# First feed-forward stage of a four-layer gated decoder: the recurrence's products, sums and ratio from VectorE to GpSimd, norms scaled by a broadcast operand, and results turned at another place in TensorE's queue

## The chip, the core and the metric

The kernel runs on one core of a Trainium2 chip. The metric is device time in microseconds (us) of one execution. The core has five instruction queues that run side by side and meet at semaphores: PE (TensorE, matmuls and transposes), DVE (VectorE), ACT (ScalarE), POOL (GpSimd) and SP (which only issues DMAs here). Each queue is in order: an instruction that waits holds up everything behind it on its own engine.

## The reference

Eight sequences (B = 8) of 256 tokens with 512 features pass four layers; each layer adds a gated attention-like part and a gated feed-forward part to `x`. The stage in question computes two additions at once:

```python
x = x + tanh(g_ffn[0])   * L0_ffn(layernorm(x), W_up, W_gate, W_down)      # 512 -> 2048 -> 512, ternary weights, silu gate
x = x + tanh(g_xattn[1]) * wkv(w, u, k=layernorm(x), v=ctx)                # after the line above
# wkv, per channel, over the 256 time steps:
no = max(o, u + k);   A = exp(o - no);      E = exp(u + k - no)
y  = (A*p + E*v) / (A*q + E)
no2 = max(w + o, k);  A2 = exp(w + o - no2); E2 = exp(k - no2)
p, q, o = A2*p + E2*v, A2*q + E2, no2
```

## The kernel before

The stage is written as one function per engine (`pool_stage12`, `pe_stage12`, `act_stage12`, `dve_stage12`, from line 793), and each engine's order is written out by hand. An outer loop runs over the 8 sequences `b`; an inner one over `j` = 0 to 7, eight slices of 256 of the 2048 hidden features. For one slice:

- PE, `up_gate(b, j)` (L829): 32 matmuls of 128x256 for the up and the gate product, into one of two pairs of PSUM banks. It waits until `hid` of slice j-2 is computed, since that frees the banks.
- ACT takes tanh of the first half (L931); DVE makes `hid` in two operations (L1066, L1068; the text calls the pair "hid j"); ACT rounds it to fp16 (L934, "high j"); DVE makes the fp16 rest (L1088, "low j"), which waits for high j.
- PE, `down(b, j)` (L816): 8 matmuls of 128x512. Down j is issued behind up_gate j+2 and waits for low j.

Between these, each slice carries pieces of three other jobs. In the pass over sequence b they are, by their place before the change:

1. Norm and keys of sequence b-1 (its feed-forward result has just been added): sums at DVE j = 0 (`norm_sums`, L749, L753), the power -1/2 on POOL (L169, L170), scaling at DVE j = 0 behind low 0 (`norm_apply`, L758, two operations for two tiles of 128 tokens), turning on PE at j = 1 and 2 (`keys`, L744), copying on ACT at j = 1 and 2 (`key_copy`, L890), then the running maximum (DVE j = 4, L1028), the differences (j = 5, L1039), ReLU and exp on ACT (j = 6, 7 and 0; L899 to L921), and the scans for q and p (L1047, L1049 at j = 7, L1058 behind the loop over j).
2. The quotient of sequence b-2: three products (`products`, L989 to L991, DVE j = 1), two sums (`totals`, L997, L999, j = 2), reciprocal in halves (`invert`, L1006, j = 3 and 6), and the ratio (L1012, j = 7).
3. The result of sequence b-3 is turned back on PE (`y_back`, L839, at j = 0 and 2) and added to x (`add_y`, L1019, DVE j = 1 and 3).

The norm of sequence b+1 for its own feed-forward pass runs beside them: sums at DVE j = 2, scaling at j = 3, the two tiles are turned on PE at j = 4 and 6 through PSUM bank 0, copied by ACT in the same j (`ffn_high`, L763) and by DVE at j = 5 and 7 (`ffn_low`, L768). All turns through bank 0 form one chain: each waits on `front_bank_free`, the count of tiles already taken out of the bank. Behind the loop over j, DVE adds the feed-forward result to x (L1108) once `down(b, 7)` is done.

After the pass over b = 7 the same jobs are finished for sequences 5 to 7 in a tail that DVE leads, up to the norm for the next stage (`NEXT`).

A few helpers: `dc.step` counts an instruction on a semaphore, `settle` waits until all counted ones are complete, `link` is both. `front_rstd` (L167) is the pair L169, L170.

Of the kernel before, what the change touches and what calls it, by code (L numbers as in the profile page):

```python
# [13 lines left out]
ALU = mybir.AluOpType  # L14
# [51 lines left out]
def build(nc, t):  # L66
# [3 lines left out]
    with ctx:  # L70
# [684 lines left out]
        def norm_apply(dve, f, xi):  # L755
            dve.wait_ge(sig("front_rstd"), f + 1)
            for t_ in range(TT):
                nc.vector.tensor_scalar(xn[:, f % 2, t_, :], X[:, xi * TT + t_, :], mv[:, t_, 0:1], rstd[:, t_:t_ + 1],  # L758
                                        ALU.subtract, ALU.mult).then_inc(sig("xn_ready"), 1)

# [32 lines left out]
        def pool_stage12(pool, pc):  # L793
            def rstd_of(f):
                front_rstd(pool, pc, None, f % 8, f // 8)

            rstd_of(front_of_ffn(0))
            for b in range(B + 2):
                if 1 <= b <= B:
                    rstd_of(front_of_wkv(b - 1))  # L800
                if b + 1 < B:
                    rstd_of(front_of_ffn(b + 1))
                if b == B:
                    rstd_of(NEXT)
                    rstd_of(NEXT + 1)

        def pe_stage12(pe):
# [41 lines left out]
            for b in range(B):  # L849
                f = front_of_ffn(b)  # L850
                pe.wait_ge(sig("front_bank_free"), tile_no(f, TT))
                for j in range(NJ):
                    if b == 0 and j < 2:
                        pe.wait_ge(sig("conv_added"), B + 3 + 2 * j)
                    if b == 0 and j == 2:
                        pe.wait_ge(sig("conv_added"), NTILES)
                    up_gate(b, j)
                    if j == 0:
                        y_back(b - 3, 0)
                    if j == 1:  # L860
                        keys(b - 1, 0)
                    if j == 2:
                        y_back(b - 3, 1)
                        keys(b - 1, 1)
                    if j in (4, 6) and b + 1 < B:
                        transpose_front(pe, front_of_ffn(b + 1), j // 2 - 2)
                    if j >= 2:
                        down(b, j - 2)
                down(b, NJ - 2)
                down(b, NJ - 1)  # L870
            y_back(B - 3, 0)
            keys(B - 1, 0)
# [10 lines left out]
        def act_stage12(act):  # L883
# [43 lines left out]
            for b in range(B):  # L927
                for j in range(NJ):
# [7 lines left out]
                    if j == 0:  # L936
                        present_exp(b - 2)
                    if j in (1, 2):
                        key_copy(b - 1, j - 1)
                    if j in (1, 2, 3, 5, 6):  # L940
                        sum_later(act, 5 * b + (1, 2, 3, 5, 6).index(j))
                    if j in (4, 6) and b + 1 < B:
                        ffn_high(act, front_of_ffn(b + 1), (b + 1) % 2, j // 2 - 2)
                    if j == 6:
# [22 lines left out]
        def dve_stage12(dve, dc, conv_add):  # L967
# [14 lines left out]

            def products(c):
                if c < 0:
                    return
                dve.wait_ge(sig("wkv_exp_ready"), 2 * c + 2)
                dve.wait_ge(sig("wkv_pq_ready"), KD * (c + 1))
                dc.settle()
                dc.step(nc.vector.tensor_tensor(wk_den, wk_d[:, 0], wk_q[:, :, 0:S], ALU.mult))  # L989
                dc.step(nc.vector.tensor_tensor(wk_num, wk_d[:, 0], wk_p[:, :, 0:S], ALU.mult))  # L990
                nc.vector.tensor_tensor(wk_ev, wk_d[:, 1], wk_v, ALU.mult).then_inc(sig("wkv_ev_ready"), 1)  # L991

            def totals(c):
                if c < 0:
                    return
                dc.settle()
                nc.vector.tensor_tensor(wk_den, wk_den, wk_d[:, 1], ALU.add).then_inc(sig("wkv_den_ready"), 1)  # L997
                dve.wait_ge(sig("wkv_ev_ready"), 2 * c + 2)
                nc.vector.tensor_tensor(wk_num, wk_num, wk_ev, ALU.add).then_inc(sig("wkv_den_ready"), 1)  # L999

            def invert(c, half):
                if c < 0:
                    return
                dve.wait_ge(sig("wkv_den_ready"), 2 * c + 2)
                part_ = wk_den[:, 2 * half:2 * half + 2, :]
                dc.step(nc.vector.reciprocal(part_, part_))  # L1006

            def ratio(c):
                if c < 0:
                    return  # L1010
                dc.settle()
                nc.vector.tensor_tensor(wk_y, wk_num, wk_den, ALU.mult).then_inc(sig("wkv_y_ready"), 1)  # L1012
# [29 lines left out]
            def weights_scan(c):  # L1042
                if c < 0:
                    return
                dve.wait_ge(sig("wkv_exp_ready"), 2 * c + 1)
                dve.wait_ge(sig("wkv_v_loaded"), 16 * (c + 1))
                nc.vector.tensor_tensor(wk_ev, wk_d[:, 3], wk_v, ALU.mult).then_inc(sig("wkv_ev_ready"), 1)  # L1047
                for k in range(KD):
# [12 lines left out]
            for b in range(B):  # L1061
                for j in range(NJ):
# [7 lines left out]
                    if j == 0 and b:  # L1070
                        dve.wait_ge(sig("ffn0_added"), TT * b + TT)
                        norm_sums(dve, dc, front_of_wkv(b - 1), b - 1)
                    if j == 1:
                        products(b - 2)
                    if j == 2:
                        totals(b - 2)
                    if j == 3:
                        invert(b - 2, 0)
                    if j == 4:
                        running_max(b - 1)  # L1080
                    if j in (5, 7) and b + 1 < B:
# [31 lines left out]
            norm_apply(dve, front_of_wkv(c), c)  # L1113
            products(c - 1)
            add_y(c - 2, 0)
            totals(c - 1)
            add_y(c - 2, 1)
# [4 lines left out]
            invert(c - 1, 1)  # L1122
            ratio(c - 1)
            dve.wait_ge(sig("wkv_added"), TT + TT * (c - 1))
# [2296 lines left out]
```

## Time and profile before

| | us |
|---|---|
| median of three runs | 3336.74 (3334.93 to 3345.0) |
| the profiled execution's own time | 3338.15 |
| its span, first to last instruction | 3336.4 |
| the stage's loop, first to last up_gate matmul | 334.0 to 735.5 |
| the stage's tail, to about | 812 |

Busy shares of the whole span are PE 87%, DVE 75%, ACT 52%, POOL 28%. They average over seven stages with different limits. The pass over one sequence takes about 50 us, and the eight passes together 12% of the span. In the timeline views a row's first number is the start in us from the span's start and the second the duration; the number in brackets is how long the engine stood idle before it, and behind the arrow whose work it waited for. Instructions on one engine overlap slightly at their ends, so that a row of 0.69 us costs its queue about 0.6.

### The profile page before, as it was taken

Reading aid. Unit: us, or ns where it says so; the run is one execution under the profiler, and the core shown is the slowest. Engines: PE = TensorE matmul, PEld = TensorE weight load, DVE = VectorE, ACT = ScalarE, POOL = GpSimd, SP = SyncE. Lnnn points to the kernel's source line nnn. Section 1 sums busy time; section 2 is a strip of 40 time slices with the busy share of each in tenths; the row PEclk is TensorE's granted clock in tenths of the full one; section 3 lists DMA queues with packets and bytes.
Section 4 is the critical chain, followed back from the end, with each engine's and each line's share of the span. In section 5 each row is a group of like instructions: output and inputs, shape, how many; then the busy total and the mean of one; then the engine's idle time right before and its main releaser. Section 6 shows DMA issues by size and latency. Waiting matters only on the chain.

```text
span 3336.4 us, 48456 instructions
## 1 busy us (share of the span) xinstructions
PE 2912.3 (87%) x18346; PEld 1702.2 (51%) x18346; DVE 2497.5 (75%) x4554; ACT 1724.1 (52%) x2659; POOL 923.7 (28%) x1359
## 2 busy tenths in 40 slices
PE   8999988883789898668888667999999999998999
PEld 4444766652444444456666433555455445444666
DVE  7887589988766666788888768777777777766433
ACT  3331344444265554079998864454444544445444
POOL 5543000002200000046776774222222222211000
PEclk9999999996899999889999878999999999999999
DMA  7422221212110102100000021000000000011000
GB/s 250 142 98 74 65 63 58 64 49 85 31 27 24 27 17 73 48 26 1 1 1 1 24 80 57 1 7 7 1 7 7 1 7 7 1 47 59 13 14 26
DMA packets 60421, 132.78 MB, mean 40 GB/s; under 512 B 6496, under 2 KB 27808, under 8 KB 59424
## 3 DMA queue, kind: packets, MB, share of 16 engines
q1 hardware_dynamic: 50976, 96.11, 9.3%
q10 hardware_dynamic: 9216, 33.56, 3.3%
q8 instruction: 150, 2.46, 0.3%
q14 instruction: 79, 0.65, 0.1%
HBM read 119.03 MB, written 4.19 MB: 37 GB/s over the span
## 4 chain that ended last, share of the span: by engine, by line
PE 60%; DVE 23%; ACT 9%; issue 4%; POOL 3%; DMA 0%; DVEq 0%; ACTq 0%; SPq 0%; POOLq 0%
PE psum L1269 10%; PE psum L660 8%; PE psum L2237 5%; PE psum L2767 4%; PE psum L3238 3%; PE psum L3216 3%; PE psum L2726 3%; ACT area_g L2312 3%; PE psum L829 3%; PE psum L2751 3%; PE psum L2118 2%; PE psum L2736 2%; PE psum L2258 2%; DVE area_a L1876 2%; PE psum L1524 2%
## 5 line engine op out<-in xcount | busy, mean ns | idle before, releaser
L2312 ACT ACTIVATE area_g<-area_a 128x2048 bf16<-128x2048 f32 x168 | 334.7, 1996 | 32.1 <-POOL area_a L2181 22.9
L2237 PE MATMUL psum<-area_c,ident_bf 128*128 128x128 bf16 x3328 | 234.2, 236 | 93.7 <-DVE area_c L2346 93.7
L660 PE MATMUL psum<-area_b,area_g 128*128 128x512 f32 x640 | 280.9, 595 | 2.1 <-issue 2.1
L2237 PEld LDWEIGHTS psum<-area_c,ident_bf 128*128 128x128 bf16 x3328 | 218.9, 107 | 119.6 <-DVE area_c L2346 112.4
L169 POOL TENSOR_TENSOR rstd<-mean_var,eps_col 128x2 f32<-128x2 f32 x56 | 19.0, 339 | 938.0 <-DVE mean_var L753 498.1
L829 PE MATMUL psum<-xT_high,area_a 128*128 128x256 f16 x1024 | 236.9, 280 | 1.4 <-DVE xT_low L768 1.4
L2726 PE MATMUL psum<-area_b,stage 128*128 128x512 f32 (+1 forms) x512 | 237.5, 546 | 0.0
L829 PE MATMUL psum<-xT_low,area_a 128*128 128x256 f16 x1024 | 236.5, 280 | 0.0
L2878 ACT ACTIVATE xn<-psum,small 128x384 f32<-128x384 f32 (+1 forms) x256 | 163.8, 640 | 96.1 <-DVE small L3017 95.9
L3017 DVE TENSOR_REDUCE small<-psum 128x1 f32<-128x384 f32 (+1 forms) x256 | 158.3, 618 | 71.6 <-PE psum L2727 69.2
L2643 POOL TENSOR_TENSOR small<-small,half_pow 128x4 f32<-128x4 f32 x96 | 131.7, 1372 | 273.9 <-DVE small L2964 273.9
L660 PEld LDWEIGHTS psum<-area_b,area_g 128*128 128x128 f32 x640 | 120.7, 191 | 148.1 <-issue 144.1
L2751 PE MATMUL psum<-area_g,area_a 128*128 128x512 f16 x672 | 166.2, 381 | 29.5 <-DVE area_g L3030 24.3
L2887 ACT ACTIVATE area_g<-psum 128x384 f16<-128x384 f32 (+1 forms) x256 | 139.3, 544 | 93.0 <-PE psum L2736 91.4
L2177 POOL TENSOR_SCALAR area_a<-area_a 128x1 f32<-128x1 f32 x224 | 130.9, 584 | 184.5 <-ACT area_g L2312 175.9
L2635 POOL TENSOR_TENSOR stage<-area_g 128x256 f32<-128x256 f32 x79 | 58.7, 742 | 441.0 <-ACT area_g L2860 311.8
L1269 PE MATMUL psum<-area_c,xT_high 128*128 128x512 f16 x512 | 178.7, 391 | 0.0
L1876 DVE TENSOR_REDUCE area_a<-psum 128x2 bf16<-128x512 f32 x256 | 163.4, 682 | 15.7 <-PE psum L1483 15.4
L479 POOL TENSOR_TENSOR area_b<-area_b,area_c 128x512 f32<-128x512 f32 x128 | 139.6, 1122 | 118.5 <-PE psum L660 112.5
L3023 DVE RECIPROCAL small<-small 128x1 f32<-128x1 f32 x256 | 41.6, 163 | 168.3 <-ACT xn L2878 165.4
L2736 PE MATMUL psum<-ident,xn 128*128 128x128 f32 x896 | 145.7, 280 | 19.8 <-DVE xn L3024 19.0
L3030 DVE SCALAR_TENSOR_TENSOR area_g<-psum,area_g 128x384 f16<-128x384 f32 (+1 forms) x256 | 157.9, 617 | 0.8 <-ACT area_g L2887 0.8
(423 smaller groups left out, 7490.7 us busy)
## 6 DMA issues: line engine op xcount, KB each, us to landing
stage<-in_w ACTq DMA_DIRECT2D x24, 512.0 KB, 4.4
stage<-in_w SPq DMA_DIRECT2D x24, 512.0 KB, 3.6
area_g<-in_toeplitz SPq DMA_DIRECT2D x32, 256.0 KB, 2.7
area_b<-in_ctxT SPq DMA_DIRECT2D x15, 512.0 KB, 3.9
area_b<-area_b SPq DMA_DIRECT2D x24, 256.0 KB, 3.7
stage<-in_ctxT SPq DMA_DIRECT2D x9, 512.0 KB, 4.0
x_stream<-in_x SPq DMA_DIRECT2D x4, 1024.0 KB, 8.1
area_c<-in_ctxT SPq DMA_DIRECT2D x8, 512.0 KB, 7.5
```

The costliest lines, as they stand in the source:

```text
L660: last = nc.tensor.matmul(psum[:, bank + m, :], toep[:, h % 2, (m - k) * P:(m - k + 1) * P], kv[:, h % 2, k, :], start=(k == 0), stop=(k = ...
L829: last = nc.tensor.matmul(out, w[:, k, m * P:(m + 1) * P], xt[:, b % 2, k, :], start=(k == 0 and n == 0), stop=(k == KD - 1 and n == 1))
L1269: r = nc.tensor.matmul(out, u, v, start=(first and n == 0), stop=(last_ and n == 2))
L1876: nc.vector.tensor_reduce(max4[:, st % 2, 4 * u + 2 * n:4 * u + 2 * n + 2], src, AX.X, ALU.max, negate=True).then_inc(sig("max4_ready"), 1)
L2237: last = nc.tensor.matmul(psum[:, 1, t_ * P:(t_ + 1) * P], identb[:, :], above5[:, t_, c * P:(c + 1) * P], start=(c == 0), stop=(c == KE - 1))
L2312: nc.scalar.activation(junk5[t_], z5[b % 3][:, t_, :], ACT.Sign, bias=fine5[:, par, t_:t_ + 1], scale=-1.0, accum_out=signs5[:, t_:t_ + 1] ...
L2726: nc.tensor.matmul(psum[:, 2 + n % 2, 0:nk], qT6[:, u % 2, h, :], kT6[:, b % 2, 0:nk // P, g, :], start=True, stop=False)
L2736: last = nc.tensor.transpose(psum[:, 4 + n % 2, k * P:(k + 1) * P], p6[:, n % 2, k * P:(k + 1) * P], ident[:, :])
L2751: last = nc.tensor.matmul(psum[:, 6, :], v6[:, b % 2, k, vp, g * P:(g + 1) * P], pT6[:, pp, k, :], start=(vp + pp + k == 0), stop=(pp == 1 ...
L2878: nc.scalar.activation(p6[:, n % 2, 0:nk], psum[:, 2 + n % 2, 0:nk], ACT.Exp, bias=nmax6[:, n % 2:n % 2 + 1], scale=-1.0, accum_out=sum6[: ...
L3017: nc.vector.tensor_reduce(nmax6[:, n % 2:n % 2 + 1], psum[:, 2 + n % 2, 0:nk], AX.X, ALU.min).then_inc(sig("nmax6_ready"), 1)
L3030: nc.vector.scalar_tensor_tensor(out=pT6[:, 1, 0:nb, h * P:(h + 1) * P], in0=psum[:, 4 + n % 2, 0:nb * P].rearrange("p (n q) -> p n q", q= ...
```

## The change

POOL receives `denominator`, `numerator` and `ratio` for sequences 0 to 6 (six operations of 128x1024), placed between the two norms' powers of a pass; DVE keeps only the reciprocals, now at j = 1 and 2. For the last sequence DVE keeps the denominator and the ratio, and POOL makes the numerator. The norm's scaling is a `scalar_tensor_tensor` whose second tensor operand is `rstd` broadcast along 512 elements, where it was a `tensor_scalar`. On PE, keys move from j = 1, 2 to j = 2, 3; the turns for the next feed-forward pass from j = 4, 6 to j = 5, 6; the turn-back of tile 0 from j = 0 of the pass b+3 to the place before the last down product of the pass b+2. ACT's and DVE's partner operations move with them: `ffn_low` from j = 5, 7 to j = 6, 7, the second norm's sums and scaling from j = 2, 3 to j = 3, 4, `add_y` of tile 0 from j = 1 to j = 0.

```diff
@@ norm_apply
-                nc.vector.tensor_scalar(xn[:, f % 2, t_, :], X[:, xi * TT + t_, :], mv[:, t_, 0:1], rstd[:, t_:t_ + 1],
-                                        ALU.subtract, ALU.mult).then_inc(sig("xn_ready"), 1)
+                nc.vector.scalar_tensor_tensor(out=xn[:, f % 2, t_, :], in0=X[:, xi * TT + t_, :], scalar=mv[:, t_, 0:1],
+                                               in1=rstd[:, t_:t_ + 1].broadcast_to([P, D]), op0=ALU.subtract,
+                                               op1=ALU.mult).then_inc(sig("xn_ready"), 1)
@@ pool_stage12
+            def denominator(c):
...
+                pool.wait_ge(sig("wkv_exp_ready"), 2 * c + 2)
+                pool.wait_ge(sig("wkv_pq_ready"), KD * (c + 1))
...
+                pc.link(nc.gpsimd.tensor_tensor(wk_den, wk_d[:, 0], wk_q[:, :, 0:S], ALU.mult))
+                nc.gpsimd.tensor_tensor(wk_den, wk_den, wk_d[:, 1], ALU.add).then_inc(sig("wkv_den_ready"), 1)
+            def numerator(c):
...
+                pc.step(nc.gpsimd.tensor_tensor(wk_num, wk_d[:, 0], wk_p[:, :, 0:S], ALU.mult))
+                nc.gpsimd.tensor_tensor(wk_ev, wk_d[:, 1], wk_v, ALU.mult).then_inc(sig("wkv_ev_ready"), 1)
+                pc.settle()
+                pool.wait_ge(sig("wkv_ev_ready"), 2 * c + 2)
+                nc.gpsimd.tensor_tensor(wk_num, wk_num, wk_ev, ALU.add).then_inc(sig("wkv_den_ready"), 1)
+            def ratio(c):
...
+                pool.wait_ge(*after("wkv_inverted", 2 * c + 2))
+                pool.wait_ge(sig("wkv_den_ready"), 2 * c + 2)
...
+                nc.gpsimd.tensor_tensor(wk_y, wk_num, wk_den, ALU.mult).then_inc(sig("wkv_y_ready"), 1)
...
                 if 1 <= b <= B:
                     rstd_of(front_of_wkv(b - 1))
+                    denominator(b - 2)
+                    numerator(b - 2)
+                    ratio(b - 2)
@@ pe_stage12, behind up_gate(b, j)
-                    if j == 0:
-                        y_back(b - 3, 0)
-                    if j == 1:
-                        keys(b - 1, 0)
                     if j == 2:
                         y_back(b - 3, 1)
-                        keys(b - 1, 1)
-                    if j in (4, 6) and b + 1 < B:
-                        transpose_front(pe, front_of_ffn(b + 1), j // 2 - 2)
+                    if j in (2, 3):
+                        keys(b - 1, j - 2)
+                    if j in (5, 6) and b + 1 < B:
+                        transpose_front(pe, front_of_ffn(b + 1), j - 5)
                     if j >= 2:
                         down(b, j - 2)
                 down(b, NJ - 2)
+                y_back(b - 2, 0)
                 down(b, NJ - 1)
@@ act_stage12
-                    if j in (1, 2):
-                        key_copy(b - 1, j - 1)
+                    if j in (2, 3):
+                        key_copy(b - 1, j - 2)
...
-                    if j in (4, 6) and b + 1 < B:
-                        ffn_high(act, front_of_ffn(b + 1), (b + 1) % 2, j // 2 - 2)
+                    if j in (5, 6) and b + 1 < B:
+                        ffn_high(act, front_of_ffn(b + 1), (b + 1) % 2, j - 5)
@@ dve_stage12, between hid j and low j
-                    if j == 1:
-                        products(b - 2)
-                    if j == 2:
-                        totals(b - 2)
-                    if j == 3:
-                        invert(b - 2, 0)
...
-                    if j in (5, 7) and b + 1 < B:
-                        ffn_low(dve, (b + 1) * TT + (j - 5) // 2 + 1, (b + 1) % 2, (j - 5) // 2)
-                    if j == 6:
-                        invert(b - 2, 1)
-                    if j == 7:
-                        ratio(b - 2)
+                    if j in (6, 7) and b + 1 < B:
+                        ffn_low(dve, (b + 1) * TT + j - 5, (b + 1) % 2, j - 6)
@@ dve_stage12, behind low j
-                    if j in (1, 3):
-                        add_y(b - 3, j // 2)
-                    if j == 2 and b + 1 < B:
+                    if j in (0, 3):
+                        add_y(b - 3, j // 3)
+                    if j in (1, 2):
+                        invert(b - 2, j - 1)
+                    if j == 3 and b + 1 < B:
                         norm_sums(dve, dc, front_of_ffn(b + 1), b + 1)
-                    if j == 3 and b + 1 < B:
+                    if j == 4 and b + 1 < B:
                         norm_apply(dve, front_of_ffn(b + 1), b + 1)
```

In the tail the same functions leave DVE's queue; `last_denominator(7)` and `last_ratio(7)` stay on it, and `numerator(7)` is POOL's last piece of the stage.

## Rows read from the trace of the kernel before

**Rows 1.** The page, busy time, share and instructions of each engine over the span.

```profile
PE 2912.3 (87%) x18346; PEld 1702.2 (51%) x18346; DVE 2497.5 (75%) x4554; ACT 1724.1 (52%) x2659; POOL 923.7 (28%) x1359
```

**Rows 2.** Windows: length, busy us (instructions) of PE, PEld, DVE, ACT, POOL, clock, DMA.

```profile
334.00:384.00 50.00, 50.00 (x379) 38.07 (x380) 24.59 (x42) 17.32 (x30) 0.89 (x2) 0.96 0.20 63
484.00:534.00 50.00, 43.39 (x314) 31.40 (x313) 45.34 (x67) 24.83 (x36) 2.14 (x4) 0.97 0.20 64
```

**Rows 3.** Timeline of DVE, pass b = 3: start, us, instruction, idle before, releaser.

```profile
482.79 0.68 DVE L1066 SCALAR_TENSOR_TENSOR area_b<-area_b,psum 128x512 f32<-128x512 f32 x1
...
487.22 1.00 DVE L758 TENSOR_SCALAR xn<-x_stream,mean_var,rstd 128x512 f32<-128x512 f32 x2 [0.86 <-POOL rstd L170]
488.13 0.68 DVE L1066 SCALAR_TENSOR_TENSOR area_b<-area_b,psum 128x512 f32<-128x512 f32 x1
489.45 1.22 DVE L989 TENSOR_TENSOR area_c<-area_c,area_b 128x1024 f32<-128x1024 f32 x1
...
502.08 3.35 DVE L1006 RECIPROCAL area_c<-area_c 128x512 f32<-128x512 f32 x1
...
508.77 2.43 DVE L1028 TENSOR_TENSOR_SCAN area_b<-scalars,area_b 128x256 f32<-128x256 f32 x4
...
513.11 0.69 DVE L1066 SCALAR_TENSOR_TENSOR area_b<-area_b,psum 128x512 f32<-128x512 f32 x1 [1.33 <-PE psum L829]
...
515.22 0.69 DVE L1088 SCALAR_TENSOR_TENSOR area_b<-area_b 128x512 f16<-128x512 f32 x1
515.83 3.25 DVE L1039 SCALAR_TENSOR_TENSOR area_c<-area_b,scalars 128x256 f32<-128x256 f32 x8
...
525.08 0.69 DVE L1066 SCALAR_TENSOR_TENSOR area_b<-area_b,psum 128x512 f32<-128x512 f32 x1 [0.88 <-ACT area_b L931]
...
528.99 1.23 DVE L1047 TENSOR_TENSOR stage<-area_c,stage 128x1024 f32<-128x1024 f32 x1 [0.16 <-ACT area_c L906]
...
536.25 0.68 DVE L1066 SCALAR_TENSOR_TENSOR area_b<-area_b,psum 128x512 f32<-128x512 f32 x1
```

**Rows 4.** Timeline of PE, pass b = 3, columns as in rows 3.

```profile
487.82 0.89 PE L744 MATMUL psum<-ident,xn 128*128 128x128 f32 x4 [3.08 <-DVE xn L758]
491.72 0.27 PE L829 MATMUL psum<-xT_high,area_a 128*128 128x256 f16 x1
496.99 0.27 PE L829 MATMUL psum<-xT_high,area_a 128*128 128x256 f16 x1
500.48 1.89 PE L816 MATMUL psum<-area_a,area_b 128*128 128x512 f16 x8
507.13 0.66 PE L744 MATMUL psum<-ident,xn 128*128 128x128 f32 x4 [1.27 <-DVE xn L758]
```

**Rows 5.** Timeline of ACT, pass b = 3, columns as in rows 3.

```profile
484.76 1.89 ACT L921 ACTIVATE area_c<-area_c 128x2048 f32<-128x2048 f32 x1
514.56 0.63 ACT L934 ACTIVATE area_b<-area_b 128x512 f16<-128x512 f32 x1 [2.57 <-DVE area_b L1068]
527.07 1.89 ACT L906 ACTIVATE area_c<-area_c 128x2048 f32<-128x2048 f32 x1
```

**Rows 6.** By source line: durations ns min/median/max, first and last start.

```profile
L491 POOL TENSOR_TENSOR area_g<-area_a,area_g x16: 1259/1268/1272, 28.8 to 175.5; 128x512 f32<-128x512 f32 x16
L2635 POOL TENSOR_TENSOR stage<-area_g x79: 722/725/1701, 2005.2 to 3068.3; 128x256 f32<-128x256 f32 x79
```

**Rows 7.** Timeline of DVE and POOL where both read SBUF, three places elsewhere.

```profile
154.04 1.66 DVE L556 SCALAR_TENSOR_TENSOR x_stream<-area_g,gates,x_stream 128x512 f32<-128x512 f32 x1
154.09 1.06 POOL L479 TENSOR_TENSOR area_b<-area_b,area_c 128x512 f32<-128x512 f32 x1
155.11 1.51 POOL L479 TENSOR_TENSOR area_b<-area_b,area_c 128x512 f32<-128x512 f32 x1
...
777.80 0.96 POOL L170 TENSOR_TENSOR rstd<-rstd,half_pow 128x2 f32<-128x2 f32 x1
...
795.70 2.49 POOL L1177 TENSOR_TENSOR x_stream<-x_stream,area_g 128x512 f32<-128x512 f32 x2
```

More of the change, by code:

```diff
@@ L127, in sig, with reused, after @@
             return sems[name]
+        REUSED = {"wkv_inverted": ("kv_ready", KD * HC)}
+        def reused(name):
+            return sig(REUSED[name][0])
+        def after(name, n):
+            return sig(REUSED[name][0]), REUSED[name][1] + n
         def at(i, par, per, k):
@@ L795, in rstd_of @@
                 front_rstd(pool, pc, None, f % 8, f // 8)
+            def denominator(c):
+                if c < 0:
+                    return
+                pool.wait_ge(sig("wkv_exp_ready"), 2 * c + 2)
+                pool.wait_ge(sig("wkv_pq_ready"), KD * (c + 1))
+                if c:
+                    pool.wait_ge(sig("wkv_y_ready"), c)
+                pc.link(nc.gpsimd.tensor_tensor(wk_den, wk_d[:, 0], wk_q[:, :, 0:S], ALU.mult))
+                nc.gpsimd.tensor_tensor(wk_den, wk_den, wk_d[:, 1], ALU.add).then_inc(sig("wkv_den_ready"), 1)
+            def numerator(c):
+                if c < 0:
+                    return
+                pool.wait_ge(sig("wkv_exp_ready"), 2 * c + 2)
+                pool.wait_ge(sig("wkv_pq_ready"), KD * (c + 1))
+                if c:
+                    pool.wait_ge(sig("wkv_y_ready"), c)
+                pc.step(nc.gpsimd.tensor_tensor(wk_num, wk_d[:, 0], wk_p[:, :, 0:S], ALU.mult))
[4 more added lines that the diff above has]
+            def ratio(c):
+                if c < 0:
+                    return
+                pool.wait_ge(*after("wkv_inverted", 2 * c + 2))
+                pool.wait_ge(sig("wkv_den_ready"), 2 * c + 2)
+                if c:
+                    pool.wait_ge(sig("wkv_yT_ready"), TT * c)
+                nc.gpsimd.tensor_tensor(wk_y, wk_num, wk_den, ALU.mult).then_inc(sig("wkv_y_ready"), 1)
             rstd_of(front_of_ffn(0))
@@ L805, in pool_stage12 @@
                     rstd_of(NEXT + 1)
+            numerator(B - 1)
         def pe_stage12(pe):
@@ L869, in pe_stage12 @@
                 down(b, NJ - 2)
+                y_back(b - 2, 0)
                 down(b, NJ - 1)
-            y_back(B - 3, 0)
             keys(B - 1, 0)
@@ L981, in dve_stage12, with last_denominator @@
                 dc.step(nc.vector.memset(z[:, :, 0:1], v))
-            def products(c):
-                if c < 0:
-                    return
+            def last_denominator(c):
                 dve.wait_ge(sig("wkv_exp_ready"), 2 * c + 2)
                 dve.wait_ge(sig("wkv_pq_ready"), KD * (c + 1))
[L988 to L999, printed above, removed]
+                dve.wait_ge(sig("wkv_y_ready"), c)
+                dc.link(nc.vector.tensor_tensor(wk_den, wk_d[:, 0], wk_q[:, :, 0:S], ALU.mult))
+                dc.link(nc.vector.tensor_tensor(wk_den, wk_den, wk_d[:, 1], ALU.add))
+                dve.sem_inc(sig("wkv_den_ready"), 1)
             def invert(c, half):
@@ L1003, in invert, with last_ratio @@
                     return
-                dve.wait_ge(sig("wkv_den_ready"), 2 * c + 2)
[L1005 to L1011, printed above, removed]
+                if c < B - 1:
+                    dve.wait_ge(sig("wkv_den_ready"), 2 * c + 1)
+                part_ = wk_den[:, 2 * half:2 * half + 2, :]
+                nc.vector.reciprocal(part_, part_).then_inc(reused("wkv_inverted"), 1)
+            def last_ratio(c):
+                dve.wait_ge(*after("wkv_inverted", 2 * c + 2))
+                dve.wait_ge(sig("wkv_den_ready"), 2 * c + 2)
                 nc.vector.tensor_tensor(wk_y, wk_num, wk_den, ALU.mult).then_inc(sig("wkv_y_ready"), 1)
@@ L1046, in weights_scan @@
                 dve.wait_ge(sig("wkv_v_loaded"), 16 * (c + 1))
+                if c:
+                    dve.wait_ge(sig("wkv_den_ready"), 2 * c)
                 nc.vector.tensor_tensor(wk_ev, wk_d[:, 3], wk_v, ALU.mult).then_inc(sig("wkv_ev_ready"), 1)
@@ L1113, in dve_stage12 @@
             norm_apply(dve, front_of_wkv(c), c)
-            products(c - 1)
             add_y(c - 2, 0)
-            totals(c - 1)
             add_y(c - 2, 1)
@@ L1122, in dve_stage12 @@
             invert(c - 1, 1)
-            ratio(c - 1)
             dve.wait_ge(sig("wkv_added"), TT + TT * (c - 1))
@@ L1133, in dve_stage12 @@
             sums34(dve, dc)
-            products(c)
-            totals(c)
+            last_denominator(c)
             squares_to_pool(dve, dc)
@@ L1139, in dve_stage12 @@
             invert(c, 1)
-            ratio(c)
+            last_ratio(c)
             for t_ in range(TT):
```

## The prediction

> **What bounds the kernel now.** The page's busy shares [rows 1] average seven stages and say nothing of this one, so I went to the windows. In the pass over b = 0 PE is busy all the time, 50.0 of 50 us; in the pass b = 3 no engine is, PE 43.4 and DVE 45.3, and POOL works 2.1 us [rows 2]. A stage in which nobody is full is bound by a chain that changes engines, and that is read from the timelines, engine by engine. I take the pass b = 3 and count from its hid 0 at 482.79; the next pass's hid 0 starts at 536.25, so a pass lasts 53.46 us [rows 3]. What ends last in it:
>
> - DVE, from 0 to about 24.3: the norm, hid, products, sums and reciprocal, up to the scaling that PE waits for at 507.13 (1.27 us) [rows 4].
> - PE from 24.3 to hid 7 at 42.29: DVE waits for it twice, 1.33 us at 513.11 and 0.88 us at 525.08, there with ACT's tanh in between [rows 3].
> - From hid 7 to the next hid 0, 11.17 us: hid and low 7, then the history product L1047, the scans and the sum onto x. L1047 waits for an exp of ACT [rows 3, 5].
> - PE also loses time early on: it waits 3.08 us for the scaled norm at 487.82, and restarts at the slow one of its two levels (four turns in 0.89 us against 0.66 at 507.13), back at full speed by 491.7 [rows 4]. That is some 3.9 us at half speed, 1.9 us lost, so 5.0 in all. It is not on the chain of this pass: DVE's hid 3 comes later anyway.
>
> **Prices.** hid costs DVE 1.32 (487.22 + 1.00 to 489.45, less overlap), low 0.60 (515.22 to 515.83), a product or sum of 1024 elements 1.14 (1.22 less the overlap of 0.08), a reciprocal half 3.26, running maximum 2.35, differences 3.17 [rows 3]. up_gate costs PE 3.49 (496.99 to 500.48), a down 1.73 (1.89 less overlap), four turns 0.47 (0.66 less overlap) [rows 4].
>
> **What DVE loses and gains per pass.** Off its queue: 3 products, 2 sums, 1 ratio, 6 x 1.14 = 6.8 us. But the ratio stood where DVE would wait otherwise: with hid 7 at 525.08, high 7 and the exp at 527.07 to 528.96 [rows 5], L1047 can't start before 528.99 in either version. So the stretch from hid 7 to the next hid 0 stays 11.17, and 5.7 us remain. Against it:
>
> 1. low j waits for ACT's high j. From the start of hid to that of low are 2.11 us (513.11 to 515.22), although only 1.32 + 0.6 of work lay between [rows 3]. Before, every slice had a filler there. After, j = 1, 2, 3 and 5 have none (the reciprocals now stand behind low), and each costs 2.11 - 1.32 = 0.79 idle, 3.2 us in all.
> 2. The scaling with two tensor operands: no such row exists. The old pair cost 1.00 less overlap, 0.91 [rows 3], which is the lower end; the upper is 2 x 0.69, the row of low, which is the nearest: the same instruction, two SBUF tensors, 512 elements. It costs its queue 0.60, so I take 1.2 a pair: +0.3, twice a pass.
> 3. The scaling for the next feed-forward pass moves behind hid 4, running maximum and low 4, and behind both reciprocals instead of one.
>
> **POOL's six operations.** None of 128x1024 is in the trace. Two inputs of 512 elements take 1.268 us, of 256 elements 0.725 [rows 6]: 0.543 per 256 more, so 1.268 + 2 x 0.543 = 2.35 us. Bounds: 2.1 (twice the 1.06 of L479 in rows 7) and 2.6. Six are 14.1 us on an engine that has 2.1 us of work, and the quotient isn't needed before the next pass. By load this is free; the price is what they do to DVE. The Trainium skill (GPSIMD Engine Reference, Instruction dispatch) gives some 2.5 cycles an element at 1.2 GHz for two inputs; my estimate from it is 2.13 us, and the sum would shrink by a tenth.
>
> **DVE and POOL exclude each other.** At 154.04 DVE's L556, which reads two SBUF tensors, takes 1.66 us; it ends with 0.6 us of work behind POOL's L479, which ran from 154.09 to 155.15, and POOL's next one, started at 155.11, takes 1.51 instead of 1.06 [rows 7]. Each was held for the other's whole instruction, then they alternate: L170 at 777.80, among four scans of DVE, takes 0.96, one scan's rest and not four. L1177 meanwhile runs twice in 2.49, full speed, beside a reciprocal of DVE [rows 7]: one with a single input doesn't count. The Trainium skill (SBUF — State Buffer, Who interferes with whom) has this as a rule: a DVE instruction with two SBUF inputs contends with a GpSimd one that reads SBUF, and the first holds the pair of ports for the whole instruction. It speaks against this change, as the new scaling falls under it just as the old did; the trace agrees, with the 1.66 us.
>
> Which DVE work meets POOL's? Scaling (two SBUF tensors), low (two), not hid or add_y (PSUM and SBUF), not the reciprocal. POOL is free at 4.4, when its power is done (that releases the scaling, at 487.22, rows 3), and the exp it needs ended before that, 484.76 + 1.89 = 486.65 [rows 5]. The walk, with POOL's work P1 to P6:
>
> - If DVE's scaling takes the pair first: scaling 0 4.43-5.05, P1 5.05-7.4, scaling 1 7.4-8.0, P2 8.0-10.35, add_y and hid 1 from 8.0 to 10.0, low 1 wanted at 10.8, held by P3 until 12.7, ends 13.3, reciprocal to 16.6, hid 2 and low 2 to 19.3, reciprocal to 22.5, hid 3, low 3 wanted at 24.6, held by P6 until 24.95, ends 25.55.
> - If P1 is first: scaling 0 held until 6.75, scaling 1 until 9.75 (P2 gets in between), low 1 until 15.1, low 3 ends at 27.95.
> - Without exclusion low 3 ends at 21.24 by the same walk.
>
> So exclusion costs 4.3 or 6.7 us a pass. P1 and the scaling are released by the same instruction, so I can't say which wins.
>
> **What PE does.** It no longer waits for the keys at j = 1. But a turn through bank 0 waits for the tile before it to leave the bank. Turn 1 of the next pass stands behind up_gate 6; tile 0 leaves with `ffn_low` at DVE's j = 6, behind hid 6, and hid 6 waits for up_gate 6. Before, `ffn_low` was at j = 5, a slice ahead. PE now stands still from the end of up_gate 6 until hid 6 and ffn_low are done: 0.3 + 1.32 + 0.68 = 2.3 us, in every pass with a next one, and up_gate 7 and hid 7 with it.
>
> From low 3 on: add_y 0.66, sums 1.58, hid 4, maximum, low 4, 6.5 to the scaling, at 27.75 without exclusion, PE's turn at 28.5, its queue has waited 2.4 us. hid 5, low 5, differences: DVE reaches hid 6 at 34.83; PE has finished up_gate 6 at 34.2. ffn_low ends 36.8, turn 1, down 4, up_gate 7: 36.9 + 0.47 + 1.73 + 3.49 = 42.6, hid 7 at 42.84. Before it was 42.29. So without exclusion a pass lasts 54.0, +0.5: what DVE saves it spends waiting, 5.3 us of it before hid 7. With exclusion it is 58.3 or 60.7, +4.8 or +7.2.
>
> **The sum.** b = 0, PE-bound: +2.3 (turn 1). b = 1, no quotient yet: the 3.08 + 1.9 before the keys go, turn 1 costs 2.3, other waits 0.7: -2. b = 2 to 6: 5 x 4.8 = 24 or 5 x 7.2 = 36. b = 7 has no next pass, so neither turn 1 nor the second scaling to wait for: the 4.3 or 6.7 of exclusion less some 3.5 that DVE sheds there, +1 or +3. Tail: DVE sheds 6 x 1.14 for sequence 6 and 3 x 1.14 for sequence 7, 10.3 us, but its scans and differences, all with two SBUF inputs, alternate with P1 to P5 of 2.35 each from 751 on, and the product L1047 with the ratio: I take 0, between -6 and +6. Sum: 2.3 - 2 + 24 + 1 = +25 or 2.3 - 2 + 36 + 3 = +39, middle +32. On the profiled execution's 3338.15 that is 3370; its time is 1.4 above the runs' median, so against them **3369**, with 3354 to 3382 as this case's own range.
>
> **The rivals.**
>
> - *Exclusion is short* (POOL lets DVE in between its reads, or the long tiles fall into gaps): the walk with 54.0 a pass, b = 2 to 6 5 x 0.5, b = 7 -3.5, b = 0 and 1 nothing together: -1, about 3336. For it: a held DVE was only seen with 512-element tiles. Against: 1.66 for 0.6.
> - *PE was the bound, faster*: PE gets back the 5.0 us before the keys in each pass from 1 to 7 and DVE's 5.7 us let it. It holds if DVE reaches hid 6 and ffn_low early enough that the chain is DVE's alone: 53.46 - 5.7 + 0.6 + 3.2 less its waits for PE and tanh of 1.33 and 0.88 is 49.4 a pass, -4.1 in six: -25, 3312. It decides from where turn 1's wait is shorter than 2.3 minus what PE is ahead. Against: that wait is set by hid 6 of the same slice, whatever DVE's load.
> - *The clock falls as well*: PE waits 2.7 us or more before turn 0 and 3.5 before turn-back 1; at 3.08 it came back slow [rows 4]. 1.75 us more in each of five passes on top of P1 first: 39 + 9 = +48, 3385.
>
> **Chances.** Forecast 0.52, short exclusion 0.2, PE the bound 0.17, clock 0.11. The runs tell no change within 0.3%, 10 us. Slower by more: 0.51 of the first, all of the last, little of the second: 0.64. Within: 0.18. Faster: 0.18. Range 3322 to 3387; what it leaves out is most of the faster rival.
>
> **What would show it.** Rows on POOL of about 2.35 us; DVE's scaling and low 1 with durations of 1.5 to 3 us instead of 0.6 (if they stay 0.7, exclusion is refuted); PE idle 2.3 us at the second turn, released by ffn_low L768; no 3.08 us wait at keys; 5 us of DVE idle before hid 7; spacing of hid 0 near 58 to 61 us. A spacing under 53 refutes the forecast.

## The result, and the profile after

The changed kernel takes 3396.63 us (median of 4 runs, 3394.83 to 3398.03) against 3338.22 us for the kernel before, measured beside it. The ratio is 1.0172 with a 95% interval of 1.0160 to 1.0184: slower by 58 us, where I had forecast slower by 32 (3369, range 3322 to 3387). The direction was right, the size was not, and the time lies outside the range.

The spans differ by 59.8 us (3396.2 against 3336.4). The page after, busy us and shares as in [rows 1]:

```profile
PE 2933.0 (86%) x18346; PEld 1710.0 (50%) x18346; DVE 2507.1 (74%) x4509; ACT 1723.3 (51%) x2659; POOL 1037.2 (31%) x1404
```

POOL has 113 us more. DVE lost 45 instructions and is busy *longer*, 2507.1 against 2497.5 us: time in which it is held counts as busy. That is the first thing to see; the busy share of a held engine hides the wait.

DVE's timeline, one pass (b = 3) from hid 0 at 498.62 (start, us, instruction, idle before); it answers to [rows 3]:

```profile
498.62 0.68 DVE L1102 SCALAR_TENSOR_TENSOR area_b<-area_b,psum 128x512 f32<-128x512 f32 x1
...
503.06 5.39 DVE L768 SCALAR_TENSOR_TENSOR xn<-x_stream,mean_var,rstd 128x512 f32<-128x512 f32 x2 [0.87 <-POOL rstd L180]
508.37 0.74 DVE L1053 SCALAR_TENSOR_TENSOR x_stream<-psum,gates,x_stream 128x512 f32<-128x512 f32 x1
...
511.12 2.23 DVE L1114 SCALAR_TENSOR_TENSOR area_b<-area_b 128x512 f16<-128x512 f32 x1 [0.70 <-ACT area_b L978]
513.28 3.34 DVE L1041 RECIPROCAL area_c<-area_c 128x512 f32<-128x512 f32 x1
...
524.50 1.02 DVE L1114 SCALAR_TENSOR_TENSOR area_b<-area_b 128x512 f16<-128x512 f32 x1 [0.70 <-ACT area_b L978]
...
531.91 1.41 DVE L768 SCALAR_TENSOR_TENSOR xn<-x_stream,mean_var,rstd 128x512 f32<-128x512 f32 x2
...
548.88 0.69 DVE L1102 SCALAR_TENSOR_TENSOR area_b<-area_b,psum 128x512 f32<-128x512 f32 x1 [6.99 <-PE psum L876]
```

The same scaling pair L768 takes 5.39 us at 503.06, beside POOL's work, and 1.41 at 531.91, without it. Low 1 (511.12) takes 2.23 and low 3 1.02, where a free one takes 0.69. The reciprocal is 3.34 as before. Then DVE stands idle 6.99 us before hid 7.

POOL in that pass; of these rows only the power L180 has a counterpart before. The products, sums and the ratio are the prediction's P1 to P6:

```profile
502.32 0.70 POOL L180 TENSOR_TENSOR rstd<-rstd,half_pow 128x2 f32<-128x2 f32 x1
502.99 2.17 POOL L815 TENSOR_TENSOR area_c<-area_c,area_b 128x1024 f32<-128x1024 f32 x1
505.24 2.67 POOL L816 TENSOR_TENSOR area_c<-area_c 128x1024 f32<-128x1024 f32 x1
507.86 2.62 POOL L825 TENSOR_TENSOR area_c<-area_c,area_b 128x1024 f32<-128x1024 f32 x1
510.46 2.35 POOL L826 TENSOR_TENSOR stage<-area_c,stage 128x1024 f32<-128x1024 f32 x1
512.95 2.62 POOL L829 TENSOR_TENSOR area_c<-area_c,stage 128x1024 f32<-128x1024 f32 x1
522.61 2.36 POOL L838 TENSOR_TENSOR area_g<-area_c 128x1024 f32<-128x1024 f32 x1 [7.05 <-DVE area_c L1041]
```

POOL's first product starts at 502.99, before the scaling that the same power released (503.06): P1 went first. The 5.39 us are P1 to 505.16, scaling 0, P2 to 507.91, scaling 1. Undisturbed P2, P4, P5 and P6 take 2.35 to 2.36 and P3 takes 2.17 (as in number 7), so that P2 and P5 carry 0.3 and P3 0.45 us of waiting for DVE.

PE, same pass, to [rows 4] (turn 0 and turn 1 are the transposes of the two tiles of the next feed-forward norm):

```profile
509.26 1.09 PE L886 MATMUL psum<-ident,area_g 128*128 128x128 f32 x4 [5.51 <-DVE x_stream L1053]
...
532.71 0.66 PE L754 MATMUL psum<-ident,xn 128*128 128x128 f32 x4 [2.46 <-DVE xn L768]
533.20 1.89 PE L863 MATMUL psum<-area_a,area_b 128*128 128x512 f16 x8
...
541.25 1.08 PE L754 MATMUL psum<-ident,xn 128*128 128x128 f32 x4 [2.67 <-DVE xT_low L779]
542.13 3.15 PE L863 MATMUL psum<-area_a,area_b 128*128 128x512 f16 x8
```

PE waits 5.51 us for add_y (before: 3.08 for the keys), 2.46 at turn 0 and 2.67 at turn 1, released by ffn_low L779. Behind the last of these the eight down matmuls take 3.15 us instead of 1.89. The windows behind turn 1 and behind turn 0 (columns as in [rows 2]) show why: granted clock 0.51, the slower of the two levels, against 1.00.

```profile
541.25:544.70 3.45, 3.45 (x11) 1.72 (x12) 0.64 (x1) 3.28 (x5) 0.00 (x0) 0.51 0.50 152
532.71:536.00 3.29, 3.29 (x22) 2.24 (x23) 2.56 (x5) 1.33 (x2) 0.00 (x0) 1.00 0.06 17
```

The slow stretch behind turn 1 is on the chain, since DVE has nothing left to do before hid 7. The one behind the 5.51 us is not: DVE starts hid 3 at 522.45 without a wait for PE.

The profile's view of the chain that ended last passes the sums of the keys' norm in every pass, so their starts in that view give the pass lengths. Before and after, for b = 2 and b = 3:

```profile
432.64 1.21 DVE stats L749 x2
484.19 1.21 DVE stats L749 x2
...
537.65 1.21 DVE stats L749 x2
```

```profile
438.78 1.21 DVE stats L759 x2
...
500.02 1.21 DVE stats L759 x2
...
561.44 1.21 DVE stats L759 x2
```

51.55 and 53.46 us before, 61.24 and 61.42 after. All of it in one table, read from the same chain:

| stretch | before | after | more | forecast, P1 first |
|---|---|---|---|---|
| start of the loop | 334.0 | 336.3 | +2.4 | 0 |
| b = 0 up to the sums | 49.7 | 52.0 | +2.3 | +2.3 |
| b = 1 | 48.95 | 50.46 | +1.5 | -2 |
| b = 2 | 51.55 | 61.24 | +9.7 | +7.2 |
| b = 3 to 6, each | 53.5 | 61.4 | +7.9 | +7.2 |
| b = 7 | 49.8 | 53.9 | +4.1 | +3 |
| tail, to the sums at 814.05 and 870.61 | 65.9 | 71.0 | +5.1 | 0 |
| the rest of the kernel | | | +3.2 | 0 |

The tail's rows show the holds once more. On the chain stand two scaling pairs of 5.41 and 5.31 us (1.41 without POOL's work, as number 1 below shows), the running maximum with 5.31 (2.44) and the history product with 2.07 (1.22), 11.6 us in all:

```profile
802.40 5.41 DVE L768 SCALAR_TENSOR_TENSOR xn<-x_stream,mean_var,rstd 128x512 f32<-128x512 f32 x2 [1.09 <-POOL rstd L180]
811.22 5.31 DVE L1062 TENSOR_TENSOR_SCAN area_b<-scalars,area_b 128x256 f32<-128x256 f32 x4 [0.73 <-ACT area_b L934]
```

### The profile page after: what moved, and what is told of

Same layout as the page of the kernel before. It is cut to its first block, busy times and chain, and to the rows that moved or that the text cites. A ratio compares the mean times of both kernels' runs of the same rounds, so it can differ in the third digit from the quotient of the medians.

```text
span 3396.2 us, 48481 instructions
## 1 busy us (share of the span) xinstructions
PE 2933.0 (86%) x18346; PEld 1710.0 (50%) x18346; DVE 2507.1 (74%) x4509; ACT 1723.3 (51%) x2659; POOL 1037.2 (31%) x1404
## 3 DMA queue, kind: packets, MB, share of 16 engines
q8 instruction: 150, 2.46, 0.3%
## 4 chain that ended last, share of the span: by engine, by line
PE 57%; DVE 25%; ACT 9%; issue 5%; POOL 2%; DMA 0%; DVEq 0%; ACTq 0%; SPq 0%; POOLq 0%
PE psum L1293 10%; PE psum L670 8%; PE psum L2261 5%; PE psum L2791 4%; PE psum L3262 3%; PE psum L3240 3%; ACT area_g L2336 3%; PE psum L2750 3%; PE psum L2775 3%; PE psum L2142 3%; PE psum L2760 2%; PE psum L2282 2%; DVE area_a L1900 2%; PE psum L876 2%; PE psum L1548 2%
## 5 line engine op out<-in xcount | busy, mean ns | idle before, releaser
L876 PE MATMUL psum<-xT_high,area_a 128*128 128x256 f16 x1024 | 228.7, 274 | 3.2 <-DVE xT_low L779 1.4
L876 PE MATMUL psum<-xT_low,area_a 128*128 128x256 f16 x1024 | 228.4, 274 | 0.0
L978 ACT ACTIVATE area_b<-area_b 128x512 f16<-128x512 f32 x64 | 40.3, 630 | 233.2 <-DVE area_b L1104 233.2
```

The lines of the kernel that those rows point to most:

```text
L876: last = nc.tensor.matmul(out, w[:, k, m * P:(m + 1) * P], xt[:, b % 2, k, :], start=(k == 0 and n == 0), stop=(k == KD - 1 and n == 1))
```

## The experiments

Times are medians; ratios are against the kernel before measured alongside, with 95% intervals. "Pass" is the length of a pass from b = 3 on. Each edit is on the changed kernel unless it says otherwise.

**1. POOL's operations made tiny** (same instructions, waits and places).

```diff
-pc.link(nc.gpsimd.tensor_tensor(wk_den, wk_d[:, 0], wk_q[:, :, 0:S], ALU.mult))
+pc.link(nc.gpsimd.tensor_tensor(wk_den[:, :, 0:1], wk_d[:, 0, :, 0:1], wk_q[:, :, 0:1], ALU.mult))
...
```

> The changed kernel, with POOL's six operations of a pass cut to one column of each 256 (128x4 elements instead of 128x1024); all waits and places stay. The rest of each tile of numerator, denominator and y is left out, so y is not the recurrence's. Theory (POOL's long operations hold DVE, 6 to 7 us a pass, and PE's turn waits are the rest): the scaling pair falls from 5.4 to 1.3 us, low 1 from 2.2 to 0.7, low 3 from 1.0 to 0.7, a pass from 61.4 to about 54 to 55.5, the time from 3397 to about 3350 (6 passes x 6.5, and some 5 of the tail). Rival (the moved turns on PE are the cause, POOL's work hides beside them): a pass stays near 60, the time above 3385.

3346.08 us, ratio 1.0014 (1.0004 to 1.0023), passes of 53.9 and 55.5. So the length of POOL's operations makes about 50 of the 58 us. DVE's scaling in it:

```profile
496.01 1.41 DVE L768 SCALAR_TENSOR_TENSOR xn<-x_stream,mean_var,rstd 128x512 f32<-128x512 f32 x2 [0.86 <-POOL rstd L180]
...
500.10 0.69 DVE L1114 SCALAR_TENSOR_TENSOR area_b<-area_b 128x512 f16<-128x512 f32 x1 [0.70 <-ACT area_b L978]
```

1.41 instead of 5.39 and low 1 0.69 instead of 2.23, with the same instructions queued. The passes are near the walk without exclusion, 54.0; the granted clock is 0.97 in the passes of 53.9 and 0.94 in those of 55.5. With DVE relieved of the whole quotient and POOL costing next to nothing, a pass is no shorter than before, nor than with the moved places alone (54.9, number 5). The same with the places left as before was not run. The tail is 59.3 us here, 6.6 less than before and 11.7 less than after.

**2. POOL waits for the scaling.**

```diff
                     rstd_of(front_of_wkv(b - 1))
+                    pool.wait_ge(sig("xn_ready"), tile_no(front_of_wkv(b - 1), TT - 1))
                     denominator(b - 2)
```

> The changed kernel, where POOL's first product of a pass waits until DVE has scaled both tiles of the keys' norm (one wait more on POOL, before denominator). Theory (who takes the ports first decides): the scaling pair takes 1.3 instead of 5.4 us, keys and hid 1 come 4 us earlier, but low 1 and low 2 now meet P2 and P5, so a pass gains about 2 of them: 59.5 us, time about 3385. Rival (each held instruction simply moves to the next one, the sum of held time is constant): no gain, 3397. Rival 2 (all 4 us stay gained): 3373.

3379.67 us, ratio 1.0119 (1.0102 to 1.0136): 17 us gained, passes of 57.6 and 59.0. Between the theory's 12 and rival 2's 24. DVE:

```profile
496.51 1.41 DVE L768 SCALAR_TENSOR_TENSOR xn<-x_stream,mean_var,rstd 128x512 f32<-128x512 f32 x2 [0.87 <-POOL rstd L180]
...
500.60 2.57 DVE L1115 SCALAR_TENSOR_TENSOR area_b<-area_b 128x512 f16<-128x512 f32 x1 [0.70 <-ACT area_b L979]
...
508.40 2.17 DVE L1115 SCALAR_TENSOR_TENSOR area_b<-area_b 128x512 f16<-128x512 f32 x1 [0.70 <-ACT area_b L979]
```

The scaling is free, low 1 is held 0.3 longer than in the changed kernel and low 2, free there (0.69), now meets P5: 4.0 gained, 1.8 handed back.

**3. Turn 1 a slice later**, which leaves its PSUM bank time to be emptied.

```diff
-                    if j in (5, 6) and b + 1 < B:
-                        transpose_front(pe, front_of_ffn(b + 1), j - 5)
+                    if j in (5, 7) and b + 1 < B:
+                        transpose_front(pe, front_of_ffn(b + 1), (j - 5) // 2)
... (ACT the same; ffn_low of tile 1 behind low 7)
```

> The changed kernel with the turn of tile 1 of the next feed-forward norm behind up_gate 7 instead of up_gate 6 (PE and ACT at j = 7), its ffn_low behind low 7. Tile 0's ffn_low at j = 6 is then done before PE reaches the turn. Theory: PE's 2.67 us wait before the second turn and the slow clock behind it (down 4 in 3.15 instead of 1.89) go, 3.5 to 4 us in each of seven passes with a next one, less 0.6 for the copy now ahead of the exp: 3.2 x 7 = 22, time about 3375, DVE's idle before hid 7 falls from 7.0 to about 3. Rival (the stretch from hid 7 to the next hid 0, with scans on DVE, sets the period): under 5 us gained.

3374.68 us, ratio 1.0098 (1.0081 to 1.0115): 22 us, as expected, with passes of 57.8 to 59.0. DVE's idle time before hid 7 falls from 6.99 to 2.82 us. The pass b = 1, which has no quotient, falls from 50.5 to 47.0: 3.5 us for this one wait and the slow clock behind it.

**4. The old form of the scaling.**

```diff
-nc.vector.scalar_tensor_tensor(out=xn[...], in0=X[...], scalar=mv[...], in1=rstd[...].broadcast_to([P, D]), ...)
+nc.vector.tensor_scalar(xn[...], X[...], mv[...], rstd[...], ALU.subtract, ALU.mult)
```

> The changed kernel with the norm's scaling as tensor_scalar again. Theory (both forms are held by POOL alike; the form costs 0.2 to 0.4 us a pair more): scaling pair beside POOL still about 5 us, other pairs 1.0 instead of 1.4, time 0.4 x 8 + 0.4 x 8 + some 3 in the next stage less, if on the chain: 3390. Rival (the new form is what is held, the old one passes): the pair takes 1.0 beside POOL, a pass gains 4, time about 3370.

3387.90 us, ratio 1.0140 (1.0124 to 1.0157), 9 us less than the changed kernel. Free pairs are 1.00, the held one is still long:

```profile
497.65 4.86 DVE L768 TENSOR_SCALAR xn<-x_stream,mean_var,rstd 128x512 f32<-128x512 f32 x2 [0.87 <-POOL rstd L180]
```

The new form bought nothing beside POOL and costs 0.4 a pair everywhere else, also in the next stage. The row also corrects a reading of the prediction, that an instruction "with a single input doesn't count": this form reads one tensor beside its two columns of scalars, and it is held all the same. What the reciprocals show holds for the reciprocals.

**5. The moved places alone** (on the kernel before: keys at j = 2, 3, turns at 5, 6, turn-back 0 before the last down product, partners with them).

> The kernel before with only the places moved (keys to j = 2, 3, the next norm's turns to j = 5, 6, turn-back 0 before the last down product, the DVE and ACT partners with them); products, sums, reciprocals and ratio stay on DVE at their old places, scaling as before. Theory (the turns' waits are a cost of their own): PE waits for ffn_low before its second turn, 2.3 to 2.7 us with a slow clock behind it, and the second scaling stands a slice later; a pass lasts 55.5 to 57 instead of 53.5, time about 3352. Rival (the moved places cost only together with POOL's work): 3340. Rival 2 (PE's 3.08 us wait at the keys was on the chain): below 3330.

3348.81 us, ratio 1.0027 (1.0016 to 1.0038): +9, a pass of 54.9 as against 53.5. PE waits 2.46 us at turn 1 for ffn_low here too. Both rivals, 3340 and below 3330, are refuted.

**6. POOL's work alone** (on the changed kernel: all places back, reciprocals at j = 3 and 6, ratio behind the second norm's power).

> The changed kernel with all places on PE, ACT and DVE as before the change (keys at j = 1, 2, turns at 4, 6, reciprocals at j = 3, 6 between hid and low, ratio on POOL behind the second norm's power); POOL's six operations and the new scaling stay. Theory (exclusion alone): the scaling pair takes 5.4 us, low 1 about 2.5, keys' turn on PE comes later by 2.4; DVE saves 5.7 but loses 4 + 2 + 1.6 (two slices without filler) in the first half: a pass of 54 to 55.5, time 3345 to 3350 with 5 from the tail. Rival (DVE's relief pays once the turns are back): a pass of 51, time 3325. Sum test: if the two parts add up, this and the run with the turns alone make up the 58 us.

3371.97 us, ratio 1.0096 (1.0079 to 1.0113): +32, a pass of 57.6. I expected +7 to +12. PE:

```profile
493.81 1.11 PE L754 MATMUL psum<-ident,xn 128*128 128x128 f32 x4 [6.13 <-DVE xn L768]
```

I had left out what the held scaling does to PE at the old places: it stands still 6.13 us and comes back slow, and DVE then waits 2.25 us at hid 3 and 1.13 at hid 5 for it. Parts 5 and 6 are +9 and +32, together 41 of 58, so they don't add. Why the other 17 appear only when both are there was not tested; my guess is that at the new places less work of DVE stands where a hold could be absorbed.

**7. The same with POOL waiting for the scaling.**

> As the run before, and POOL's first product waits until DVE has scaled both tiles. Theory: the scaling pair is back at 1.3 to 1.4 us, a pass gains 2 to 3 of the 4 us; time 3328 to 3338, no slower than the kernel before. Rival (held time only moves): as the run before.

3352.09 us, ratio 1.0036 (1.0024 to 1.0049): 20 us gained on number 6, but outside the 3328 to 3338 that I expected, and slower than before. Its passes from b = 3 on are 53.0 to 54.3 us, as long as before, although 5.7 us of work a pass are gone from DVE: in b = 3 it waits for PE instead, 2.79 us at hid 2, 0.73 at hid 3 and 1.13 at hid 5. Another 5.4 us are the tail, 71.3 against 65.9.

**8. Numbers 2 and 3 together.**

> The changed kernel with both repairs: POOL waits for the scaling, and turn 1 of the next norm stands behind up_gate 7. Alone they gave 17 and 22 us. Theory (two stretches of one chain, the first ends at the second scaling, the other at hid 7): they add, 3358. Rival (same slack): 3372.

3359.27 us, ratio 1.0059 (1.0042 to 1.0076), passes of 55.55. 37 us gained where the two alone gave 17 and 22: within 2 us they add, as two stretches of one chain do.

**9. POOL's operations in halves** (12 of 128x512 a pass).

```diff
-pc.link(nc.gpsimd.tensor_tensor(wk_den, wk_d[:, 0], wk_q[:, :, 0:S], ALU.mult))
+for k in (0, 2):
+    pc.step(nc.gpsimd.tensor_tensor(wk_den[:, k:k + 2], wk_d[:, 0, k:k + 2], wk_q[:, k:k + 2, 0:S], ALU.mult))
+pc.settle()
...
```

> The changed kernel with each of POOL's operations in two halves (12 of 128x512 instead of 6 of 128x1024 a pass; same elements, same places). Theory (DVE is held for one whole POOL instruction): each hold is at most 1.27 instead of 2.35 us, so the scaling pair takes about 3.4 instead of 5.4, low 1 at most 2.0; a pass gains 2 to 3 although POOL works 1 us more, time about 3382. Rival (the two engines share by elements, so the held time goes with POOL's load): scaling pair stays at 5.4 or grows, time 3397 or more.

3391.28 us, ratio 1.0153 (1.0138 to 1.0169), where I expected 3382. The mechanism is confirmed and the time is not: the pair takes 3.24,

```profile
498.97 3.24 DVE L768 SCALAR_TENSOR_TENSOR xn<-x_stream,mean_var,rstd 128x512 f32<-128x512 f32 x2 [0.87 <-POOL rstd L180]
```

held by two instructions of half the size instead of 5.39, though POOL moves the same elements. So DVE waits for whole instructions, not for a share. But a pass is still 61.0 (59.3 for b = 6). PE waits 3.66 us at turn 0 instead of 2.46, and the granted clock of the 2 us from turn 0 is 0.50, 0.60, 0.71 and 0.81 in the passes b = 3 to 6, where it is 1.00 in the changed kernel. DVE then waits 1.16 us for PE before hid 6, where it didn't wait. For b = 3:

```profile
526.94 1.11 PE L754 MATMUL psum<-ident,xn 128*128 128x128 f32 x4 [3.66 <-DVE xn L768]
527.85 3.13 PE L873 MATMUL psum<-area_a,area_b 128*128 128x512 f16 x8
...
536.75 0.70 PE L754 MATMUL psum<-ident,xn 128*128 128x128 f32 x4 [2.27 <-DVE xT_low L779]
537.24 3.55 PE L873 MATMUL psum<-area_a,area_b 128*128 128x512 f16 x8
```

**10 to 12. Repairs of the kernel before**, without POOL. Number 10 puts the second norm's scaling between hid 3 and low 3 and the first reciprocal half behind low 3. Number 11 moves keys, turn-back 0 and add_y 0 as the change did, but leaves the turns at j = 4 and 6. Number 12 is both:

```diff
 dve:                if j == 3:
-                        invert(b - 2, 0)
+                        norm_apply(dve, front_of_ffn(b + 1), b + 1)      # b + 1 < B
... behind low 3:
-                        norm_apply(dve, front_of_ffn(b + 1), b + 1)
+                        invert(b - 2, 0)
-                    if j in (1, 3):
-                        add_y(b - 3, j // 2)
+                    if j in (0, 3):
+                        add_y(b - 3, j // 3)
 pe:                 if j == 2:
                         y_back(b - 3, 1)
+                    if j in (2, 3):
+                        keys(b - 1, j - 2)
... (y_back(b - 2, 0) before down(b, 7); key_copy at j = 2, 3)
```

> The kernel before, with the next norm's scaling between hid 3 and low 3 (it fills the wait for high 3) and the first half of the reciprocal behind low 3. Theory (DVE's way to that scaling ends before PE's wait of 1.27 us at turn 0): the wait goes, hid 5 and hid 7 come 1.3 us earlier, 7 passes: time about 3331. Rival (DVE's stretch up to the next hid 0 absorbs it): 3340.

> The kernel before, with keys on PE and ACT at j = 2, 3 and turn-back 0 before the last down product, add_y 0 at j = 0, as in the change; the next norm's turns stay at j = 4, 6. Theory: PE's 3.08 us wait at the keys and the slow clock behind it go, but only 0.8 us of it (hid 3's wait for PE) is on the chain; 6 x 0.8 = 5 gained, time about 3335. Rival (PE's queue sets the period): 5 us a pass, 3310.

> Both of the two before. Theory: with PE early and DVE early DVE is the bound, the pass is its work without waits, about 50.5 instead of 53.5: 7 x 3 = 20 gained, time about 3320. Rival (they repair the same slack): 3331.

Number 10: 3335.95 us, ratio 0.9987 (0.9978 to 0.9996), about half of the 9 us expected, with passes of 52.0. Number 11: 3339.70, 0.9995 (0.9986 to 1.0004), no change in the sum: the 5 us that PE lost at the keys in [rows 4] were off the chain in the passes with a quotient. Only b = 1 and b = 7 are shorter, by 1.9 and 2.8 us. Of the passes b = 3 to 6 three are longer, 54.2 with a granted clock of 0.97, and b = 4 is 52.6 with 1.00. Number 12: **3325.44 us, ratio 0.9961 (0.9948 to 0.9975)**, faster than both kernels, a pass of 51.15, where I expected 3320 and 50.5. In its windows (length; busy us and instructions of PE, PEld, DVE, ACT, POOL; clock; DMA) DVE is nearly full, against 45.3 in [rows 2]:

```profile
484.00:534.00 50.00, 45.71 (x336) 33.04 (x335) 47.99 (x70) 23.69 (x36) 1.59 (x4) 0.97 0.20 64
```

## Why the prediction was wrong

**Right.** That a pass is bound by a chain and not by DVE's load: number 1, at the moved places, takes the whole quotient off DVE at next to no price and gains nothing. That DVE and POOL hold each other for whole instructions and alternate; the walk of the P1-first branch put the end of low 3 at 27.95 after hid 0, it was at 26.9 (525.52 - 498.62). That miss of 1.05 is there by the end of low 1, at 14.73 instead of 15.7: P1 and P3 took 2.17 instead of 2.35, and the two scalings kept POOL 0.3 and 0.45 us from its work where the walk had 0.6 each. That turn 1 waits for hid 6 and ffn_low. DVE's waits for high j: 0.70 in the rows, 0.79 in the forecast with overlap. POOL's 2.35 us. b = 0 came out at its +2.3. The Trainium skill's rule on the shared ports (SBUF — State Buffer, Who interferes with whom) was the right one to weigh; the traces agree, with 5.39 us for the pair of scalings in the changed kernel, 1.41 in numbers 1 and 2 and 3.24 in number 9.

**The steps that failed**, with what each makes of the 28 us between the forecast's +32 and the +60 of the two traces (1 us more is in b = 7):

1. *Who goes first* (7 us): "P1 and the scaling are released by the same instruction, so I can't say which wins", and then the middle of two sums, +25 and +39. P1 won in all seven cases, each time starting 0.07 us before the scaling (502.99 against 503.06 above). P1 starts before the power's row ends (503.02), the scaling after it. [rows 7] had the hint, L479 starting at 155.11 before its predecessor ended: POOL's next instruction is queued right behind the one that frees the rival, while the rival waits for a semaphore. With that branch alone the forecast is 3376.
2. *The tail* (5 us): "I take 0, between -6 and +6". It was +5.1. Number 1 splits it: DVE's relief is worth -6.6 and not the 10.3 of work that it sheds, the holds +11.7.
3. *The slow clock* (8 us in b = 2 to 6, of which another miss hides 5): it was a rival at 0.11, and the forecast's walk took PE as fast behind its wait at turn 1. Down 4 takes 3.15 and the four turns 1.08, together 1.7 us more a pass than with a full clock, and they are on the chain. The walk's 1.05 us too much before low 3 hid most of it: a pass was 61.4 where the walk had 60.7. The clock rival, +48, came closer than the forecast, but it placed the slow stretches elsewhere, at turn 0 and turn-back 1. Turn 0 stayed fast and turn-back 1 was off the chain.
4. *Passes taken for b = 3* (about 5 us): for b = 1, "-2", I took the 3.08 us wait and the slow clock from the pass b = 3. In b = 1 the wait was 1.66 us and PE stayed fast, so the pass got 1.5 us longer. And b = 2 lasted 51.6 us before and not 53.5, so the same new pass is 2 us more there.

```profile
387.32 0.66 PE L744 MATMUL psum<-ident,xn 128*128 128x128 f32 x4 [1.66 <-DVE xn L758]
```

5. *Outside the stage* (6 us): the loop starts 2.4 us late and the rest behind the tail is 3.2 longer. Both are within what single executions differ by: in numbers 5, 10, 11 and 12, which leave everything outside the stage as it was, the loop starts 2.0, 2.2 and 2.0 us later and 1.2 earlier than in the trace before, and the rest is 1.8 to 7.0 us longer. So no cause in the change is shown for these, beyond the scaling's 0.4 us a pair.

The "PE was the bound" rival, 0.17, had passes of 49.4. Number 1, with POOL's work near nothing, has 53.9 and 55.5, and number 11 gains nothing. Short exclusion, 0.2, is refuted by the 5.39 us in the changed kernel and by number 9.

## What to carry to other kernels

Work that goes from VectorE to GpSimd is not off VectorE's back: price each VectorE instruction that reads two SBUF tensors, and the `tensor_scalar` of number 4 as well, at one whole GpSimd instruction if it will stand beside one. Where both are released by the same GpSimd instruction, walk the queues with GpSimd first: here it was 0.07 us ahead in all seven cases. Beside GpSimd's work the reciprocals (3.34 us) and the operations that read PSUM (hid 1: 0.67 and 0.69) took no longer than before. And before relieving an engine look whether anybody waits for its load: here another order of the same instructions (number 12) was worth 13 to 15 us, and 6.8 us a pass of work taken off VectorE at the moved places nothing.

## What the runs showed of the hardware

- A wait's length alone didn't tell whether TensorE came back slow. In the kernel before, the wait at the keys is 3.07 to 3.08 us in each pass from b = 3 on, and the four turns behind it take 0.66 in b = 4 (granted clock 1.00 over the next 3.7 us) and 1.11 in b = 5 (0.50 over 3.5 us). In number 9 turns behind a wait of 2.27 took 0.70 and the down product after them 3.55.

```profile
541.28 0.66 PE L744 MATMUL psum<-ident,xn 128*128 128x128 f32 x4 [3.07 <-DVE xn L758]
...
594.74 1.11 PE L744 MATMUL psum<-ident,xn 128*128 128x128 f32 x4 [3.08 <-DVE xn L758]
```

- A two-input float32 operation of 128x1024 on GpSimd takes 2.35 to 2.36 us; a product with an operand of 257-element rows takes 2.17: L815 in all seven cases, and L825 where nothing held it (number 7, and the tail at 840.23). Why these are the quicker ones stays open.
- Reciprocal on VectorE, 128x512, takes 3.34 us beside GpSimd's work and 3.35 without it.
